# Two 32-wide attentions: the parts of Q and K stacked in depth, one matmul per score tile

## The reference, cut to what matters

```
Xn = (X - mean) * rsqrt(var + eps) * ln_g + ln_b
Q, K, V = split_heads(Xn @ Wq + bq), split_heads(Xn @ Wk + bk), split_heads(Xn @ Wv + bv)
scores = einsum('bhqd,bhkd->bhqk', Q, K) / sqrt(32);  -inf where k > q
x = x + (softmax(scores) @ V) @ Wo + bo
```

## Time and profile before

| | us |
|---|---|
| three runs | 3508.13, 3510.62, 3510.79 |
| median | 3510.62 |
| profiled execution, span from first to last instruction | 3507.3 |
| the median less that span | 3.3 |
| TensorE busy in the span | 3093.3 |
| VectorE busy | 1950.4 |
| ScalarE busy | 1294.7 |
| GpSimd busy | 706.4 |

### The profile page before, as it was taken

One profiled execution on the slowest core, in us unless ns is written; L12 is line 12 of the kernel. 1 busy time (PEld: TensorE's weight loads), 2 busy tenths in 40 slices (PEclk: granted clock), 3 DMA queues, 4 the chain that ended last, 5 costly groups with the idle time before them and its releaser, 6 DMA issues. The chain is left out here.

```text
span 3507.3 us, 50867 instructions
## 1 busy us (share of the span) xinstructions
PE 3093.3 (88%) x19076; PEld 2335.4 (67%) x19076; DVE 1950.4 (56%) x5124; ACT 1294.7 (37%) x2672; POOL 706.4 (20%) x873
## 2 busy tenths in 40 slices
PE   6999899997999995987868875998779999989999
PEld 5777677776667663544646754776367777768887
DVE  5555387776544445323466767665577787752221
ACT  2333265555323323123322225443545555541000
POOL 1111032222101100000016761000033333313222
PEclk8999999998999997789989987999889999999999
DMA  2000031002000003021110011001300000020000
GB/s 88 2 2 2 4 124 31 29 29 79 2 1 1 1 1 123 26 72 59 66 58 4 4 50 49 1 1 34 113 1 1 1 1 1 1 99 13 13 13 13
DMA packets 66456, 106.41 MB, mean 30 GB/s; under 512 B 9379, under 2 KB 30115, under 8 KB 66085
## 3 DMA queue, kind: packets, MB, share of 16 engines
q1 hardware_dynamic: 65798, 103.07, 8.5%
q0 software_dynamic: 416, 0.10, 0.0%
HBM read 90.40 MB, written 12.85 MB: 29 GB/s over the span
## 5 line engine op out<-in xcount | busy, mean ns | idle before, releaser
L402 ACT ACTIVATE tree_value<-tree_bit,table_lut,tree_step 128x256 f32<-128x256 uint8 x496 | 275.4, 595 | 136.2 <-DVE tree_value L416 65.6
L416 DVE COPY_PREDICATED tree_value<-tree_bit,tree_value 128x256 f32<-128x256 uint8 x434 | 237.5, 553 | 135.8 <-ACT tree_value L402 107.3
L805 DVE CUSTOM_DVE_ANT_0 bank<-bank,a_causal 128x384 f32<-128x384 f32 (+3 forms) x512 | 235.3, 522 | 120.3 <-PE bank L921 120.3
L729 ACT ACTIVATE a_PT<-bank 128x512 f32<-128x512 f32 (+1 forms) x384 | 174.4, 527 | 318.1 <-PE bank L934 318.1
L101 PE MATMUL bank<-f_xT_hi,f_w_hi 128*128 128x512 f32 (+1 forms) x704 | 276.0, 392 | 8.1 <-DVE f_w_lo L1219 8.1
L102 PE MATMUL bank<-f_xT_hi,f_w_lo 128*128 128x512 f32 (+1 forms) x704 | 275.7, 392 | 0.0
L103 PE MATMUL bank<-f_xT_lo,f_w_hi 128*128 128x512 f32 (+1 forms) x704 | 275.5, 391 | 0.0
L1143 POOL CAST f_h_hi<-f_sg 128x512 fp32r<-128x512 f32 (+1 forms) x88 | 84.3, 958 | 559.6 <-DVE f_sg L1240 289.0
L1242 DVE TENSOR_TENSOR f_sg<-bank,f_sg 128x512 f32<-128x512 f32 (+1 forms) x44 | 30.4, 691 | 270.4 <-PE bank L103 270.4
L101 PEld LDWEIGHTS bank<-f_xT_hi,f_w_hi 128*128 128x128 f32 (+1 forms) x704 | 132.4, 188 | 37.5 <-issue 8.8
L103 PEld LDWEIGHTS bank<-f_xT_lo,f_w_hi 128*128 128x128 f32 (+1 forms) x704 | 132.3, 188 | 28.9
(11 more groups left out here) (468 smaller groups left out, 8046.4 us busy)
## 6 DMA issues: line engine op xcount, KB each, us to landing
f_w_raw<-in_f_w SPq DMA_DIRECT2D x11, 768.0 KB, 12.7
f_w_raw<-table_w SPq DMA_DIRECT2D x11, 768.0 KB, 11.7
tree_idx<-in_f_idx SPq DMA_DIRECT2D x62, 128.0 KB, 2.1
table_w<-tree_value SPq DMA_DIRECT2D x62, 128.0 KB, 1.7
x_res<-in_x SPq DMA_DIRECT2D x4, 1024.0 KB, 11.0
m_piece<-in_m_wq SPq DMA_DIRECT2D x2, 2048.0 KB, 12.0
m_piece<-in_m_wo SPq DMA_DIRECT2D x2, 2048.0 KB, 8.4
m_piece<-in_m_w_gate SPq DMA_DIRECT2D x2, 2048.0 KB, 11.1
```

The lines of the kernel that those rows point to most:

```text
L402: act.activation(prog.tree_value[(h + to) % 4][:, :], prog.tree_bit[h % 2][0][:, :], ACT.Identity, bias=prog.table_lut[:, 2 * k:2 * k + 1] ...
L416: dve.copy_predicated(prog.tree_value[(h + keep) % 4][:, :], prog.tree_bit[h % 2][bit][:, :], prog.tree_value[(h + other) % 4][:, :]).then ...
L729: act.activation(PT[j][:, g, :], ps[J.bank(key)][:, 0:WIDTH[j]], ACT.Exp, scale=scale).then_inc(J.frees(key), 1)
L805: last = dve.tensor_tensor_reduce(out=ps[J.bank(key)][:, col:col + n], in0=ps[J.bank(key)][:, col:col + n], in1=causal[:, T - n:T], scale= ...
```

## The change

For each head a stack of 96 partitions is made: Q stack = (Q high, Q low, Q high), K stack = (K high, K high, K low). One 96-deep matmul is then the sum of the three products. For exp eight more partitions (96 to 103) hold the two parts of minus the maximum of four heads on the Q side and a constant selector of the head, `c_heads`, on the K side, so that one 104-deep matmul also adds the maximum. The stacks are made by DMAs from one flat pair of Q and one of K, three per head and operand, issued by SP; GpSimd casts each stack in place (`ready`) and tells TensorE. Stacks are double buffered. A step is now one head with its three fills (FILLS turned round). ORDER changes: exp before max at each step, the negation ("neg") is a job of its own, the first max of the unit after next and all of pv and sum stand at the unit's end, and the pieces stand elsewhere. ScalarE's copy of the rows goes to the Q stack, eight partitions by 4 x 512. The copy O is gone; ScalarE writes to OT directly. Elsewhere only the names of some counters change.

```diff
+    flat = {kind: [prog.sb(f"{name}_{kind}_{part}", [P, T], F32R) for part in ("hi", "lo")] for kind in ("Q", "K")}
+    Qs = [prog.sb(f"{name}_Qs{i}", [P, G, T], F32R) for i in range(2)]
+    Ks = [prog.sb(f"{name}_Ks{i}", [P, G, T], F32R) for i in range(2)]
...
-    FILLS = [(j, g) for j in range(3) for g in range(G)]
+    FILLS = [(j, g) for g in range(G) for j in range(3)]
+    SHIFT = 3 * HD
+    DEPTH, FULL = SHIFT, SHIFT + 2 * G
...
+            kinds = [[[("V", b, 0)] if b else [], [("Q", b, 2)], [("Y", b - 1, 0), ("Y", b - 1, 1)], [("Y", b - 1, 2), ("Y", b - 1, 3)]],
+                     [[("Q", b, 3)], [], [], [("T", b + 1, c) for c in range(DC)]],
+                     [[("Q", b + 1, 0)], [("K", b + 1, 0)], [], [("VT", b + 1, 0)]],
+                     [[("Q", b + 1, 1)], [], [], []]][u][k]
         else:
+            kinds = [[[("Q", b, 2)], [("K", b, 2)], [("Y", b - 1, 0), ("Y", b - 1, 1)], [("Y", b - 1, 2), ("Y", b - 1, 3)]],
+                     [[("Q", b, 3)], [("K", b, 3)], [], [("T", b + 1, c) for c in range(DC)]],
+                     [[("Q", b + 1, 0)], [("K", b + 1, 0)], [("V", b + 1, 0)], [("V", b + 1, 1)]],
+                     [[("Q", b + 1, 1)], [("K", b + 1, 1)], [("V", b + 1, 2)], [("V", b + 1, 3)]]][u][k]
...
         for k in range(4):
-            if ahead:
-                ORDER.append((("max", ahead, k), 0))
             ORDER.append((("exp", (b, u), k), 0))
+            if ahead and k < 3:
+                ORDER.append((("max", ahead, k + 1), 0))
+            if ahead and k == 2:
+                ORDER.append((("neg", ahead, 0), 0))
+            if behind and k == 1:
                 ORDER.append((("bc", behind, 0), SUM_BANK))
             for i, piece in enumerate(pieces(b, u, k)):
+                ORDER.append((piece, EXP_BANK + i % 3))
+        if ahead:
+            ORDER.append((("rows", ahead, 0), ROWS_BANK))
+        if second_ahead:
+            ORDER.append((("max", second_ahead, 0), 0))
+        for j in range(3):
+            ORDER += [(("pv", (b, u), j), 0), (("sum", (b, u), j), 0)]
...
+            def stack(to, parts, g, landed):
+                strip = slice(HD * g, HD * (g + 1))
+                for i, part in enumerate(parts):
+                    sp.dma_start(to[HD * i:HD * (i + 1), g, :], part[strip, :].bitcast(F32)).then_inc(landed.sem, 16)
+            for m, at in enumerate(UNITS):
+                q_hi, q_lo = flat["Q"]
+                k_hi, k_lo = flat["K"]
+                for g in range(G):
+                    if g == 0:
+                        sp.wait_ge(*read(("Q",) + at))
+                    if m >= 2:
+                        sp.wait_ge(*full(("exp", UNITS[m - 2], 3 * g + 2)))
+                    stack(Qs_bits[m % 2], (q_hi, q_lo, q_hi), g, c_qs[g])
+                    if KC > 1 or at[1] == 0:
+                        if g == 0:
+                            sp.wait_ge(*read(("K",) + at))
+                        stack(Ks_bits[turn(at)], (k_hi, k_hi, k_lo), g, c_ks[g])
...
+            def ready(m, g):
+                if m >= len(UNITS):
+                    return
+                at = UNITS[m]
+                pool.wait_ge(*c_qs[g](0, 48 * (m + 1)))
+                pool.tensor_copy(Qs[m % 2][0:DEPTH, g, :], Qs_bits[m % 2][0:DEPTH, g, :]).then_inc(c_qready.sem, 1)
+                if KC > 1 or at[1] == 0:
+                    pool.wait_ge(*c_ks[g](0, 48 * stacked("K", ("K",) + at) + 48))
+                    pool.tensor_copy(Ks[turn(at)][0:DEPTH, g, :], Ks_bits[turn(at)][0:DEPTH, g, :]).then_inc(c_kready.sem, 1)
             for kind, at, k in ORDER:
+                if kind == "max" and unit(at) < 2 and k == 0:
+                    for g in range(G):
+                        ready(unit(at), g)
+                elif kind == "exp" and k:
+                    ready(unit(at) + 2, k - 1)
+                elif kind == "sum" and k == 0:
+                    ready(unit(at) + 2, G - 1)
...
+                    for c_stack in (c_qs if kind == "Q" else c_ks):
+                        if stacked(kind, key):
+                            act.wait_ge(*c_stack(0, 48 * stacked(kind, key)))
...
+                    rows = ps[J.bank(key)][SHIFT:FULL, :].unsqueeze(1).broadcast_to([2 * G, G, T])
+                    act.activation(Qs[unit(at) % 2][SHIFT:FULL, :, :], rows, ACT.Copy).then_inc(J.frees(key), 1)
...
+                elif kind == "max":
+                    g, stack = k, Qs[unit(at) % 2]
+                    pe.wait_ge(*c_qready(0, G * unit(at) + g + 1))
+                    pe.wait_ge(*c_kready(0, G * stacked("K", ("K",) + at) + g + 1))
+                    for j in range(3):
+                        key = (kind, at, 3 * g + j)
+                        pe.wait_ge(*vacant(key))
+                        for n, (col, t) in enumerate(S_PARTS[j]):
+                            wide_ = (t + 1) * P
+                            last = pe.matmul(ps[J.bank(key)][:, col:col + wide_], stack[0:DEPTH, g, t * P:(t + 1) * P], keys(at)[0:DEPTH, g, 0:wide_],
+                                             start=n == 0, stop=True, skip_group_check=True)
+                        last.then_inc(J.fills(key), 1)
+                elif kind == "exp":
...
+                        for n, (col, t) in enumerate(T_PARTS[j]):
+                            wide_ = (TT - t) * P
+                            pe.matmul(ps[J.bank(key)][:, col:col + wide_], keys(at)[0:FULL, g, t * P:(t + 1) * P], stack[0:FULL, g, t * P:T],
+                                      start=n == 0, stop=False, skip_group_check=True)
+                        for col, t in T_PARTS[j]:
+                            last = pe.matmul(ps[J.bank(key)][:, col:col + P], prog.mask_b[:, 1, :], prog.ident_b[:, :], start=False, stop=True,
+                                             skip_group_check=True)
+                        last.then_inc(J.fills(key), 1)
```

More of the change, by code:

```diff
@@ L533, in attention32 @@
+        second = [[("Q", 0, 1)], [("K", 0, 1)], [("V", 0, 2)], [("V", 0, 3)]]
+    UNITS = [(b, u) for b in range(NB) for u in range(DC)]
+    ROWS_BANK = EXP_BANK + 2
+    ORDER = [(("T", 0, c), c) for c in range(DC)] + [(piece, (4, 5, 6, 7)[i]) for i, piece in enumerate(first)]
     if biased:
-        ORDER.append((("const", 0, 0), 7))
+        ORDER.append((("const", 0, 0), 3))
     for k in range(4):
-        ORDER.append((("max", (0, 0), k), 0))
-        if k == 3:
-            ORDER.append((("rows", (0, 0), 0), EXP_BANK))
+        ORDER.append((("max", UNITS[0], k), 0))
@@ L539, in attention32 @@
         for i, piece in enumerate(second[k]):
-            ORDER.append((piece, EXP_BANK + (k + i + 1) % 3))
-    UNITS = [(b, u) for b in range(NB) for u in range(DC)]
+            ORDER.append((piece, EXP_BANK + (k + i) % 3))
+    ORDER += [(("neg", UNITS[0], 0), 0), (("rows", UNITS[0], 0), ROWS_BANK), (("max", UNITS[1], 0), 0)]
     for n, (b, u) in enumerate(UNITS):
         ahead = UNITS[n + 1] if n + 1 < len(UNITS) else None
+        second_ahead = UNITS[n + 2] if n + 2 < len(UNITS) else None
@@ L597, in unit, with turn, keys, stacked @@
         return at[0] * DC + at[1]
+    def turn(at):
+        return (at[0] if KC == 1 else unit(at)) % 2
+    def keys(at):
+        return Ks[turn(at)]
+    def stacked(kind, key):
+        return key[1] if kind == "K" and KC == 1 else key[1] * DC + key[2]
     def pv_done(at, j):
@@ L779, in _ @@
                     key = (kind, at, k)
[L780 removed]
+                    pair = flat[kind]
                     dve.wait_ge(*c_qk(0, QK_NO[key]))
@@ L889, in _ @@
                     last.then_inc(J.fills((kind, at, k)), 1)
-                elif kind in ("max", "exp"):
-                    b, c = at
-                    if kind == "max" and k == 0:
-                        pe.wait_ge(*read(("Q", b, c)))
-                        pe.wait_ge(*read(("K", b, c % KC)))
-                    if kind == "exp" and k == 0:
+                elif kind == "max":
[11 more added lines that the diff above has]
+                elif kind == "exp":
+                    g, stack = k, Qs[unit(at) % 2]
+                    if g == 0:
                         pe.wait_ge(*read(("rows", at, 0)))
@@ L929, in _ @@
-                    for f in some:
-                        j, g = FILLS[f]
-                        out = ps[J.bank((kind, at, f))]
-                        if kind == "exp":
-                            for col, t in T_PARTS[j]:
-                                last = pe.matmul(out[:, col:col + P], prog.mask_b[:, 1, :], prog.ident_b[:, :], start=False, stop=True,
-                                                 skip_group_check=True)
-                            last.then_inc(J.fills((kind, at, f)), 1)
+                    for j in range(3):
+                        key = (kind, at, 3 * g + j)
+                        pe.wait_ge(*vacant(key))
+                        for n, (col, t) in enumerate(T_PARTS[j]):
[6 more added lines that the diff above has]
+                        last.then_inc(J.fills(key), 1)
@@ L951, in _ @@
```

(9 more changed lines are left out.)

132 lines of the change are left out of this document (38 added, 94 removed).

## The result

| | before | after |
|---|---|---|
| median of four runs, us | 3509.44 | 3574.77 |
| lowest to highest | 3508.13 to 3510.79 | 3567.31 to 3578.73 |
| profiled span, us | 3507.3 | 3576.8 |

After over before is 1.0189, with a 95% interval of 1.0174 to 1.0203: slower by 65 us, far outside that interval. The forecast was 3501, its range ended at 3545, so the time moved the other way and out of the range.

What follows compares the result with a forecast made beforehand. TensorE was taken to set the end in both attentions (busy 363 of 385 and 432 of 458 us). Terms -93 - 8 + 52 + 14 + 8 + 14 + 4 = -9 us gave span 3498, time 3501 us, range 3466 to 3545.

Steps and rivals of the forecast that it cites:

- Step 1: Score matmuls of both attentions: stacking takes a unit from 9.0 to 6.1 us, -93 us; changes of shape -8.
- rival C: Score matmuls: weight loads not hidden behind masks and 128-column matmuls, 7.1 us a unit, +32, time 3533; chance 0.14.
- Step 2: TensorE waits exposed whole for the bank after Q and K products: 74 us in sum, +52 over before.
- Steps 3 and 4: TensorE waits for banks of V, Y and T, +7, +4, +3; waits for the negated maxima (L tile), +8.
- Step 5: Stacking path by DMA and GpSimd: mostly hidden, but GpSimd's queue delays OT low, +14, and the T casts, +4.
- the second term: Second attention: T casts queue behind the third head's stack, TensorE's max fills wait 1.3 us three times, +4.
- The starts: First unit of an attention: 24 DMAs, 11 us, hidden behind other work; 0, within -5 to +10 us.
- rival D: Stacks land late, landing of 4 us rather than 2.1 or issues of 0.8: +20, time 3521; chance 0.16.
- All waits together: Waits of Step 2, Steps 3 and 4 and Step 5 in both attentions: +52, +14, +8, +14 and +4 us.
- rival E: Granted clock in the attentions: its mean falls by 0.02 over 780 us of work, +16, time 3517; chance 0.08.

Runs made afterwards that it cites:

- Experiment 4: Changed kernel plus a list of stacked matmuls of each width, masks alone and matmul-mask pairs at the end of each attention; 3630.3 us with the added work.
- Experiment 1: Changed kernel with the Q, K, V and Y products of places 0 to 2 in the empty banks 6 and 7; 3479.9 us, 0.9922 of the kernel before.
- experiment 6: Changed kernel with the max block of the unit ahead put behind the product instead of ahead of it; 3517.3 us, 1.0020 of the kernel before.
- Experiment 9: Kernel with the edits of Experiment 1 and Experiment 2, the second unit ahead's first max ahead of the row transposes; 3432.7 us, 0.9780 of the kernel before.
- Experiment 2: Changed kernel with GpSimd's first-head stack cast behind the OT split and third-head cast behind the T casts; 3533.5 us, 1.0072 of the kernel before.
- experiment 3: Kernel before, without stacking, with only exp put ahead of max at each place; 3642.1 us, 1.0381 of the kernel before.
- experiment 7: Changed kernel with six useless matmuls into bank 6 behind each Q and K product of units after the first; 3548.5 us, 1.0111 of the kernel before.
- experiment 8: Kernel with the edits of Experiment 1 and Experiment 2, an exp head's four matmuls first, then its four masks; 3435.4 us, 0.9792 of the kernel before.

## Why the prediction was wrong

**Step 1, -101 forecast for the score matmuls and the change of shape, -78 measured.** The size of a head was near the upper bound, not the lower. In the timeline after, a max head is 0.72 us and an exp head up to 1.05 (150.78 to 151.50, 149.73 to 150.78), the shortest 0.95, together 1.7 to 1.77, so 6.8 to 7.1 a unit where 6.1 was taken: rival C's price. By the blocks that is 22 to 32 us too little, by the three parts 23. Experiment 4 shows both reasons. The row of four is 0.63 to 0.64 us, where 0.61 was taken, as the matmul of 128 columns doesn't come at half the price of 256. And three of a head's four masks stand between fp32r matmuls, at 0.13 each, the fourth behind its like at 0.055: 0.46 a head, where 0.31 was taken. The last of these prices shows in the max head behind it, 0.72 and not 0.64. Two rows of four and the masks make 1.74 a head, 7.0 a unit. The load of 0.19 us does hide behind 96-deep matmuls of 512 columns (0.23 a piece, as at full depth), and even at 128 columns the spacing of 0.11 is less than the load. By the rule of the Trainium skill (TensorE: Matmul & The Clock Gate, Part 3, "What overlaps and what doesn't") every load here would be paid on top; these rows disagree.

**Step 2, waits behind Q and K products: the mechanism right, the size nearly.** 74 us in sum were forecast, 68 measured, each 1.4 to 1.7. The rise is 44 us and not 52: the kernel before has 24 such us, since K low costs 2.6 in its first attention too, in a row that the 21.5 left out. Experiment 1 shows the bank as their cause, experiment 6 the missing max block. What I didn't ask was whether the wait has to be: two banks stood empty.

**Steps 3 and 4: right in size.** Waits for banks of V, Y and T are some 10 us more than before in the list, 14 forecast; waits for L are 13.9 us in all, 12 forecast, and 6 more than before, as the second attention had 3.3 too. Experiment 9 shows that two thirds of those in the first attention can be covered, at the price of another wait. ScalarE's row copy takes 1.87 us, and no wait for it shows.

**Step 5: the mechanism right, the second term too small.** OT low waited 12.3 us more than before in sum, 14 forecast. The waits for the maxima behind the T casts were taken as 1.3 each; in the second attention they are up to 5.2 and 15.9 in all, against 4. The timeline of GpSimd after shows the queue: stack casts that wait for their DMAs, then the T casts.

```profile
1109.95 0.61 POOL L681 CAST a_Qs<-a_bits 96x512 fp32r<-96x512 f32 x1 [2.97 <-DMA a_bits<-a_Q_hi]
1111.26 0.61 POOL L684 CAST a_Ks<-a_bits 96x512 fp32r<-96x512 f32 x1 [0.70 <-DMA a_bits<-a_K_lo]
1111.82 3.22 POOL L697 CAST a_xT_hi<-a_xT_raw 128x512 fp32r<-128x512 f32 x4
```

VectorE's split of the T tiles hangs on that row (4.14 us from 1112.46), the reads of the maxima stand behind the split, and TensorE's next max fill began at 1117.41 after 5.22 us of idle. The step named this chain but gave it 1.3 us, less than either of the two blocks in it, the casts (3.22) and the split (4.14). Experiment 2 shows the cause: with the order changed, the waits for the maxima in the second attention are 2.3 us in sum, none over 0.5. The starts cost 3.7 and 6.7 us, waits for the first stack, 10.4 where 0 was taken and 10 was the upper end. Landing was 2.0 us as assumed, so rival D fell.

**All waits together** were forecast at +92 us and are +95. **What failed is that the sum ended there: its term for the clock was nothing.** The clock was left at the level of before, with rival E at 0.02 and 0.08 of the chances. It fell by 0.05, which cost 43 us more than before. That is over half of the 78 us between the forecast for the span (-9) and the span measured (+69); step 1's 23, 3 of the waits and the 9 us outside the attentions are the rest. For these 9 I have no experiment, and the stages are unchanged; 5 of them lie in the stage behind the second attention, whose clock was 0.84 before and 0.82 after, and 0.84 or 0.85 in experiments 1, 2 and 3, where that stage was 397.7 to 399.0 us long and not 405.1.

That stalls of this length bring the clock down is what experiment 7 shows. The same kernel, with 42 waits of 1.4 to 1.7 us filled by work of nearly equal length, gains 26 us, and all of it in the clock; the 16 low stretches that stood right behind such waits are gone. It holds as well across the edits that remove waits: 1 takes 60 us of idle time away and 23 of clock, 2 takes 22 and 15, both together 94 and 36. With 6 (34 and 35) the echo is between 0.4 and 1.0 us per us of wait. That is a mean over two attentions and no constant: in single attentions it goes from 0.2 (experiments 1 and 3, the first) to 1.4 (experiment 6, the first). The rest of rival E's argument, the mean load, isn't separated by any run: experiment 7 raised the load too.

## What to carry to other kernels

A wait on TensorE, where it sets the end, costs its own length and then an echo in the clock; here 0.4 to 1.0 us for each us, taken over both attentions. A forecast that adds waits has to add that, and a change that trades work for waits at par was a loss here. When an order moves work out from behind a producer, look first for an empty bank (or buffer), before counting the wait as a price: one line was worth 95 us here. In an in-order queue put what others wait for ahead of what only arrives, and follow the delay through every engine that stands behind it; and after each removed wait or cheaper block look for the one that was next, as in experiments 8 and 9, where nearly the whole gain went into it.

## What the runs showed of the hardware

- A bf16 matmul of 128 columns costs 0.055 us among its like and 0.13 between fp32r matmuls; fp32r matmuls of 128 columns follow at 0.11 us among their like at 96 rows of depth, where 256 columns follow at 0.12.
- The clock falls in the kernel before as well, without a long stall: the pv block at 134.65 us and the sums behind it last until 138.09. The windows of before there show the granted clock (behind the engines' busy times):

```profile
134.00:136.00 2.00, 2.00 (x19) 0.84 (x21) 0.83 (x6) 1.36 (x3) 0.00 (x0) 0.71 0.04 8
136.00:138.00 2.00, 2.00 (x36) 1.49 (x28) 0.00 (x0) 0.00 (x0) 0.00 (x0) 0.50 0.00 0
```

  Ahead of it stands only the 0.40 us of the earlier trace rows. Why a wait of 0.4 us is followed by 1.2 GHz here, and the one of 1.41 us that ends at 156.71 in the changed kernel is not until the next wait has begun, is open.
- 64 KB from SBUF to SBUF, 32 rows onto 32 rows, landed in 2.0 us at the median, 624 times in the changed kernel.
